# The normalised x1 written by VectorE instead of ScalarE

## Time and profile before

| | |
|---|---|
| median of 3 runs | 215.74 us (214.9 to 217.49) |
| span of the profiled execution | 212.6 us, 3825 instructions |
| the profiled execution's own time | not given apart from its span |
| TensorE's granted clock | 0.998 of 2.4 GHz over the span |
| instructions: DVE, ACT, POOL | 501, 234, 140 |

### The profile page before, as it was taken

How to read it: one execution, slowest core, us unless ns; L and a number is a source line. 1 busy time by engine, 2 the same in 40 slices (tenths; PEclk the granted TensorE clock), 3 DMA queues, 4 the chain that set the end, 5 groups by cost and what they waited for, 6 DMA issues and landing times.

```text
span 212.6 us, 3825 instructions
## 1 busy us (share of the span) xinstructions
PE 192.1 (90%) x1126; PEld 155.6 (73%) x1126; DVE 146.2 (69%) x501; ACT 103.2 (49%) x234; POOL 112.1 (53%) x140
## 2 busy tenths in 40 slices
PE   0896699999989899999988989999999999999992
PEld 0352556656767677888677979899999898889882
DVE  3679999999999977866535767946645333247553
ACT  3423464983567499773414556556653223122320
POOL 6002504357598787667720077777767777760000
PEclk9999999999999999999999999999999999999999
DMA  5999993000100101111125446621111110039243
GB/s 166 309 390 259 177 378 153 5 0 25 39 28 27 38 25 41 52 38 50 52 63 112 106 118 149 158 59 43 47 33 38 45 47 0 0 91 327 81 161 135
DMA packets 17607, 21.59 MB, mean 102 GB/s; under 512 B 3224, under 2 KB 11679, under 8 KB 17332
## 3 DMA queue, kind: packets, MB, share of 16 engines
q1 hardware_dynamic: 13872, 15.73, 26.4%
q0 software_dynamic: 2560, 4.24, 6.3%
q10 hardware_dynamic: 1156, 1.39, 1.9%
HBM read 13.95 MB, written 8.44 MB: 105 GB/s over the span
## 4 chain that ended last, share of the span: by engine, by line
PE 29%; DVE 28%; POOL 16%; issue 12%; DMA 8%; ACT 5%; POOLq 1%; ACTq 0%; DVEq 0%
POOL y_back L352 14%; PE bank L1222 8%; DVE qkv L757 7%; DMA y_back<-yg,xg 6%; DVE ss L765 4%; DVE st L719 4%; PE quad_banks L1200 3%; PE quad_banks L1202 3%; PE quad_banks L1201 3%; PE quad_banks L1115 3%; ACT h_rows L471 2%; DVE rn L770 2%; DMA w_qkv<-w_in 2%; PE quad_banks L1245 2%; DVE mv L722 2%
## 5 line engine op out<-in xcount | busy, mean ns | idle before, releaser
L352 POOL DMA_INDIRECT y_back<-yg,xg x48 | 47.3, 985 | 30.5 <-ACT yg L543 15.0
L842 DVE TENSOR_TENSOR s_act<-quad_banks,sg_act 128x512 f32<-128x512 f32 x32 | 22.0, 688 | 26.9 <-PE bank L1222 15.3
L515 ACT ACTIVATE sg_act<-quad_banks 128x512 f32<-128x512 f32 x32 | 19.2, 599 | 42.1 <-PE quad_banks L1202 42.1
L343 POOL DMA_INDIRECT x_slots<-h_rows,pos x32 | 31.6, 988 | 12.2 <-issue 6.2
L1222 PEld LDWEIGHTS bank<-sdT,s_act 128*128 128x128 f32 x256 | 31.8, 191 | 1.7
L1222 PE MATMUL bank<-sdT,s_act 128*128 128x128 f32 x256 | 32.9, 276 | 0.0
L317 POOL TENSOR_TENSOR qkv<-qkv,rn 128x512 f32<-128x512 f32 x16 | 17.0, 1079 | 28.0 <-DVE rn L770 27.9
L1115 PE MATMUL quad_banks<-w_c,xT 128*128 128x384 f32 x64 | 25.9, 544 | 2.0 <-DVE qkv L757 1.2
L1245 PE MATMUL quad_banks<-w_gu,xgT 128*128 x96 | 22.9, 382 | 0.8 <-ACT xgT L526 0.8
L1115 PEld LDWEIGHTS quad_banks<-w_c,xT 128*128 128x128 f32 x64 | 12.6, 212 | 11.3 <-issue 4.4
L1245 PEld LDWEIGHTS quad_banks<-w_gu,xgT 128*128 128x128 f32 x96 | 17.3, 190 | 2.9 <-issue 1.0
(11 more groups left out here) (142 smaller groups left out, 364.5 us busy)
## 6 DMA issues: line engine op xcount, KB each, us to landing
xg<-x_slots SPq DMA_DIRECT2D x48, 65.0 KB, 2.0
xT<-x_t SPq DMA_DIRECT2D x8, 256.0 KB, 7.1
xres<-L_attn_x SPq DMA_DIRECT2D x8, 256.0 KB, 7.2
w_gu<-gate_up SPq DMA_DIRECT2D x1, 2048.0 KB, 14.7
h_rows<-y_back SPq DMA_DIRECT2D x8, 256.0 KB, 5.0
x_slots<-zeros SPq DMA_DIRECT2D x1, 1040.0 KB, 16.8
w_dn<-down SPq DMA_DIRECT2D x1, 1024.0 KB, 16.7
out<-xres SPq DMA_DIRECT2D x4, 256.0 KB, 2.2
```

The source lines that it names most:

```text
L343: g.indirect_dma_start(out=x_slots, out_offset=bass.IndirectOffsetOnAxis(ap=pos[:, t:t + 1], axis=0), in_=h_rows[:, t, :], in_offset=None) ...
L352: nc.gpsimd.indirect_dma_start(out=y_back, out_offset=bass.IndirectOffsetOnAxis(ap=xg[:, n, D + 1:D + 2].bitcast(I32), axis=0), in_=yg[:, ...
L515: a.activation(sg_act[:, n % 2], pair[:, 2 * (n % 2)], ACT.Silu).then_inc(s_silu, 1)
L842: v.tensor_tensor(s_act[:, n % 2], pair[:, 2 * (n % 2) + 1], sg_act[:, n % 2], ALU.mult).then_inc(s_act_rdy, 1)
```

## The change

VectorE's `h_scales` becomes `normalise`: after the reciprocal it writes the four tiles of `h_rows` itself, `(x1 - mean) x reciprocal`, with the mean and the reciprocal as column operands of one `tensor_scalar` per tile. The column `nm2`, its four operations per block, ScalarE's `norm_h` and the semaphore `rstd2` are gone. `normalise(c)` stands in VectorE's list where `h_scales(c)` stood, for each of the eight blocks; `norm_h(c)` is taken out of ScalarE's list in eight places.

```diff
-            def norm_h(c):
-                act.wait_ge(rstd2, c + 1)
-                act.wait_ge(x1_rdy, c + 1)
-                for t in tiles(c):
-                    last = a.activation(h_rows[:, t, 0:D], xres[:, t, :], ACT.Identity, bias=nm2[:, t:t + 1],
-                                        scale=rs2[:, t:t + 1])
-                last.then_inc(h_rdy, 1)
...
-            def h_scales(c):
+            def normalise(c):
                 t = slice(Q * c, Q * c + Q)
                 dve.wait_ge(std2, c + 1)
                 link(v.reciprocal(rs2[:, t], rs2[:, t]))
                 for n in tiles(c):
-                    last = v.tensor_scalar(nm2[:, n:n + 1], mv2[:, n, 0:1], rs2[:, n:n + 1], -1.0, ALU.mult, ALU.mult)
-                last.then_inc(rstd2, 1)
+                    last = v.tensor_scalar(h_rows[:, n, 0:D], xres[:, n, :], mv2[:, n, 0:1], rs2[:, n:n + 1],
+                                           ALU.subtract, ALU.mult)
+                last.then_inc(h_rdy, 1)
...
-            norm_h(0)
...
-            h_scales(0)
+            normalise(0)
             x1_stats(1)
             take(4, 0)
             take(4, 1)
             x_stats(7)
-            h_scales(1)
+            normalise(1)
             mask_vk(1)
             weights_lo(0)
...
```

More of the change, by code:

```diff
@@ L67, in build_block @@
         rs1 = sb("rs1", [P, NT])
-        nm2 = sb("nm2", [P, NT])
         st2 = sb("st2", [P, NT, 6])
@@ L177, in build_block @@
         qT_mm, qT_sb, y_mm, x1_rdy = sem("qT_mm"), sem("qT_sb"), sem("y_mm"), sem("x1_rdy")
-        var2, std2, rstd2, h_rdy = sem("var2"), sem("std2"), sem("rstd2"), sem("h_rdy")
+        var2, std2, h_rdy = sem("var2"), sem("std2"), sem("h_rdy")
         w_hi, w_lo, log_mm = sem("w_hi"), sem("w_lo"), sem("log_mm")
@@ L572, in _ @@
             hT_hi(0)
-            norm_h(1)
             std_x(6)
@@ L584, in _ @@
             x1_copy(3)
-            norm_h(2)
             head_norms(5)
@@ L594, in _ @@
             wb_copy(2)
-            norm_h(3)
             x1_copy(4)
@@ L601, in _ @@
             x1_copy(5)
-            norm_h(4)
             hT_hi(3)
@@ L608, in _ @@
             wb_copy(3)
-            norm_h(5)
             x1_copy(6)
@@ L616, in _ @@
             x1_copy(7)
-            norm_h(6)
             std_h(7)
             hT_copy(6)
-            norm_h(7)
             silu_shared(2)
@@ L955, in _ @@
             choose(1)
-            h_scales(2)
+            normalise(2)
             head_sums(5)
@@ L963, in _ @@
             take(6, 1)
-            h_scales(3)
+            normalise(3)
             choose(2)
@@ L975, in _ @@
             choose(3)
-            h_scales(4)
+            normalise(4)
             inv_norms(7)
@@ L980, in _ @@
             mask_vk(3)
-            h_scales(5)
+            normalise(5)
             choose(4)
@@ L986, in _ @@
             choose(5)
-            h_scales(6)
+            normalise(6)
             place(5)
             x1_stats(7)
-            h_scales(7)
+            normalise(7)
             act_shared(1)
```

## The result

The changed kernel takes 225.34 us (median of 4 runs, 224.39 to 226.87) against 215.32 us before; the ratio is 1.0477, 95% interval 1.0419 to 1.0536. It is 10 us slower, where the forecast was 3.4 us slower, 219.1 us, with a range that ended at 222.5.

What follows compares the result with a forecast made beforehand. VectorE was taken to set the pace from 28 to 73 us, TensorE being full after. The terms 1.0 + 1.1 + 1.0 + 0.5 + 1.1 - 0.8 - 0.5 gave +3.4 us, forecast 219.1 us, range 214.3 to 222.5.

Steps and rivals of the forecast that it cites:

- Own time, 0.24 us a block: VectorE, each block: four operations of 268 ns replace columns of 207; 1.0 us for blocks 0 to 3, at most 1.8.
- "I take 0" for the second column: VectorE's new operation: the second column operand, for the mean, costs between 0 and 53 ns; 0 taken.
- Rival D: VectorE's new operation runs at 343 ns, not 268, with no collision: +1.7 us, 217.4 us; chance 0.08.
- The collisions: VectorE's SBUF-to-SBUF operations and POOL's exclude each other, so the later waits; terms 1.1, 1.0, 0.5, 1.1 and -0.8 us.
- Block 0: At 36.70 us POOL begins two operations, 2.12 us; VectorE waits between 0 and 2.1 us, 1.1 taken.
- Block 1: The first line 783 begins after POOL's `hT_lo` and waits for its rest: 1.0 us, between 0 and 1.3.
- Blocks 2 and 3: VectorE waits for a POOL scatter, 0.5 us, up to 1.5, and for POOL's hold from 58.67, 1.1, up to 3.1.
- the list: VectorE waits beside POOL, block by block: normalise in blocks 0, 2, 3, both lines 783, one scatter each in blocks 4 to 7.
- The second line 783 (`weights_lo`), -0.8 us: VectorE, held 1.57 us by POOL before the change, mostly waits less wherever it lands: -0.8 us, between -1.57 and 0.
- under the 1.4 us of cover: Blocks 4 to 7: VectorE's extra 0.24 us and about one scatter's wait each hide behind ScalarE's former 1.65 us; costed at nothing.
- ScalarE's relief, -0.5 us: From 73 to 92 us, ScalarE freed of `norm_h` gives back 0.5 of 0.9 us, ends 0 and 0.9.
- its 0.9 us: From 73 to 92 us, TensorE's waits for `h_rows` and `hT_full`, 0.9 us together; no more than that comes back.

Runs made afterwards that it cites:

- yield_after: The changed kernel with five waits on POOL that let VectorE go first where it was held, all work kept: 218.27 us, 1.0142.
- yield_before: The kernel before with one wait on POOL, `hT_lo(2)` behind the second `weights_lo`: 213.72 us, 0.9928.
- one_col: The changed kernel with the mean left out, so that normalise has one column operand, the reciprocal alone: 225.43 us, 1.0417.
- fill_after: The changed kernel with 27 extra 128x128 matmuls, read by nobody, in three stretches where TensorE stands still: 223.43 us, 1.0385.
- dummy_reduce: The kernel before with four unread VectorE sums over 184 numbers behind the columns of each of blocks 0 to 3: 224.29 us, 1.0424.
- fill_reduce: The kernel before with four unread VectorE sums in each of blocks 0 to 3 and 17 extra matmuls in TensorE's idle stretches: 220.89 us, 1.0239.
- yield_last: The kernel before with blocks 4 to 7 normalised by VectorE and POOL's `hT_lo(2)` and `scale_q(7)` made to wait for VectorE: 214.96 us, 0.9982.

## Why the prediction was wrong

The direction and the main mechanism held: VectorE sets the pace from 28 to 73 us, the four operations are held by POOL, and the holds are the larger part. The sizes did not hold, and one mechanism, the clock, was missing. The runs split the loss in three steps: `yield_after` against `yield_before`, 2.1% or 4.6 us, is VectorE's own time with the clock's part that is left in `yield_after` (its run at a clock of 0.999 is 3.0 us above `yield_before`, not 4.6); the change against `yield_after`, 3.4% or 7.2 us, is the holds with all that follows from them; and `yield_before` shows that 0.7%, 1.6 us, of these holds were there before. The steps share their ends, so that they add up to the measured 10 us (4.6 + 7.2 - 1.6) proves nothing by itself; each stands on its own two runs.

Step by step:

- **Own time, 0.24 us a block, "I take 0" for the second column.** This step failed. The four operations take 1.14 us in place of 0.58, 0.56 a block. Line 890 with its one column was the right row for one column, as `one_col`'s 268 shows; the second column costs 60 to 75 ns, above the 53 that was kept as the end. The term was 1.0 us for blocks 0 to 3 and is 2.2; with blocks 4 to 7, and the clock's part, the runs give 4.6 in the end. Rival D had the 343 ns, but without the collisions.
- **The collisions.** They were there, but few in their places and sizes. Block 0: 1.57, with 1.1 taken and 2.1 as the end; POOL's second operation went ahead of VectorE's second. Block 1: 0.92 where 1.0 was forecast, but that is luck: it is not line 783 (before) that waits, the longer operations themselves ran into `hT_lo`. Blocks 2 and 3: 0.5 and 1.1 taken, next to nothing measured. In block 2 one operation waits 0.21 us for the end of the scatter that began at 56.63, yet the row of four is no longer than block 3's; in block 3 POOL's operation was nearly done.
- **A hold that was not on the list:** `choose(2)`'s scan, 1.51 us. It has two inputs in SBUF, as `weights_lo` has, and only stood clear of `hT_lo(1)` by the old timing. The list looked at the changed operations and at line 783, where it should have taken every VectorE operation with two SBUF inputs that moves.
- **The second line 783 (`weights_lo`), -0.8 us.** It is held for 1.58 us as before. POOL's `hT_lo(2)` moved with it, so it met the same operation. In sum the terms to 73 us were 3.9 and measured 2.2 + 1.57 + 0.92 + 1.51 = 6.2; `incl` of block 3, which began at 72.60 before, begins at 79.57, 7.0 later, of which 0.6 is VectorE's wait at 50.34 us for a TensorE at its low clock.

```profile
72.60 0.29 DVE L799 TENSOR_TENSOR_SCAN incl<-run_mask,hot 128x64 f32<-128x64 f32 x1
```

- **Blocks 4 to 7 "under the 1.4 us of cover".** This step failed too. The prediction named what would end the cover, a wait of over 1.4 us in one block, and block 5 had it, 1.51 us behind a scatter and the tensor operation that follows it at once. The cover was also drawn for the wrong waiter: ScalarE's 1.65 us covers `turn_h`, but `choose(4)` stands behind `normalise(5)` on VectorE, and TensorE waits for its `incl`. From 79.57 on the delay grows from 7.0 to 10 us.
- **The clock.** This step is missing: the sum put the clock at nothing, and took a microsecond of VectorE for a microsecond at the end. After its new waits TensorE ran at half its clock, three times for 3.4 us, and worked off at that rate what had piled up: 2 to 3.5 us in the changed kernel (`fill_after`), and 4 us in `dummy_reduce` against `fill_reduce`, where 5 us of VectorE time, 4.0 of sums and a hold of 1.0, became 8.8.
- **ScalarE's relief, -0.5 us.** `yield_last` is the best case for it, and is 0.5% slower than `yield_before`, so whatever the relief gave was less than VectorE's own time took; and TensorE's wait for `h_rows`, which was to be gone, is still there once, 0.47 us at 39.44. The 4.9 us that the chain gave to `h_rows` were not for the taking: TensorE was full behind them, as the prediction argued with its 0.9 us.

The rule of the Trainium skill (SBUF — State Buffer, "SBUF: two separate sides"), that the later of the two engines waits to the end of the earlier, fits the holds in blocks 0 and 1, where POOL's operation began first or, at 36.68, at the same time: VectorE's end 0.1 us after POOL's. In block 5, the scan and `suT` it is not so simple. There VectorE's operation began 0.4 to 0.7 us before POOL's tensor operation, behind a scatter, and waited for both; it ended 0.1, 0.16 and, for the larger `suT`, 0.56 us after POOL. Open is why POOL goes first there, why a scatter holds VectorE in its last part only (0.21 us of 0.96 in block 2), and why an operation with two columns, which at 343 ns is no faster than line 876's from PSUM (that one reads a second tensor, too), is held at all; no run took these apart. Open too is how much of the 7.2 us is the holds themselves, 5.5 new ones by the trace, and how much the clock after them; `fill_after` gives 2 to 3.5 us for the latter, with intervals that overlap.

## What to carry to other kernels

Before an elementwise step moves to VectorE, list every VectorE operation from SBUF with two inputs or of the new kind, and lay POOL's operations beside them: in these traces where two of them met it was mostly VectorE's that waited, and a moved microsecond on a full VectorE shifted which ones met. Such a hold can be taken away by letting POOL wait for a semaphore where POOL has room; here one wait made the old kernel 0.7% faster, and five took back 7 of the 10 us. And where TensorE is nearly full, cost a new wait of its own with more than its length, for its clock may fall after it, as it did here. A trace shows one run: in `fill_after` and `yield_after` the other runs had a lower mean clock than the profiled one, and took longer.

## What the runs showed of the hardware

- A `tensor_scalar` of 128x128 in SBUF takes 268 to 283 ns with one column operand and 343 with two (`one_col`).
- A sum with one SBUF input, 334 ns, was never held by POOL (330 to 335 over 16, `dummy_reduce`), while operations with two columns or two SBUF inputs were held for up to 1.5 us (1872 ns in place of 343 in the changed kernel's block 5).
- A VectorE operation that waits behind a POOL scatter may wait through the tensor operation that POOL begins right after it, too: 66.98 to 68.78 us behind one of 66.37 to 67.33 and one of 67.35 to 68.62.
- TensorE's granted clock was 0.55 and 0.60 from 48 to 52 us after waits of 1.43 and 2.01 us, and did not fall there in the profiled run of `fill_after`, where matmuls that nobody reads filled those waits.
